# Expert weights by one register-addressed transfer per tile, and weights packed into few loads, in a two-layer macaron transformer block

## The reference

```python
x = x + 0.5 * _L0_ffn_ref(_layernorm(x), ...)    # attention, then 8 experts of which each token uses one
x = x + _L0_attn_ref(_layernorm(x), ...)         # causal attention, 16 heads of 8
x = x + 0.5 * _L0_ffn_ref(_layernorm(x), ...)    # the same weights as the first
x = x + 0.5 * _L1_ffn_ref(_layernorm(x), ...)    # dense FFN 128 -> 512 -> 128, low-rank addition, twice
x = x + _L1_attn_ref(_layernorm(x), ...)
x = x + 0.5 * _L1_ffn_ref(_layernorm(x), ...)

def _L0_ffn_ref(x, ...):
    hn = _layernorm(x, ln1_g, ln1_b)
    ...                                          # attention without a mask, 16 heads of 8, added to x
    hn2 = _layernorm(x, ln2_g, ln2_b).reshape(-1, h)
    idx = jnp.argmax(hn2 @ gate_w + gate_b, axis=-1)
    mid = relu(einsum('th,ehf->etf', hn2, w1) + b1[:, None, :])    # w1: 8 x 128 x 512
    y = einsum('etf,efh->eth', mid, w2) + b2[:, None, :]           # w2: 8 x 512 x 128
    return x + y[idx, arange(tokens)].reshape(b, s, h)
```

## Time and profile before

| | |
|---|---|
| time, median of 3 runs | 1058.04 us (1056.2 to 1064.72) |
| span of the profiled execution, first to last instruction | 1059.5 us |
| instructions | 25454 |
| TensorE matmul busy | 913.9 us (86%) |
| VectorE busy | 783.4 us (74%) |
| ScalarE busy | 676.3 us (64%) |
| GpSimd busy | 341.6 us (32%) |
| mean granted TensorE clock | 0.952 |

### The profile page before, as it was taken

The page is one execution under the profiler, slowest core; times in us unless marked ns, Lnnn a source line. Parts: engine busy times, 40 slices in busy tenths (PEclk is TensorE's granted clock), DMA queues, the critical chain, the costliest instruction groups (busy, mean ns, idle before and its releaser), DMA issues.

```text
span 1059.5 us, 25454 instructions
## 1 busy us (share of the span) xinstructions
PE 913.9 (86%) x10040; PEld 486.6 (46%) x10040; DVE 783.4 (74%) x1424; ACT 676.3 (64%) x1471; POOL 341.6 (32%) x603
## 2 busy tenths in 40 slices
PE   2599999898768799999999998987798889899997
PEld 1122333235757445554323332357675544555464
DVE  4789989964436977888999999635555697878646
ACT  2188877777546477777798876875452147767631
POOL 3444411342646323323233313426451032301100
PEclk9689999999969899999999999999798989999999
DMA  6123482001122321121021100101211122110000
GB/s 190 41 55 90 102 175 34 13 12 45 54 70 82 84 58 33 38 64 41 24 57 28 42 3 12 38 18 42 79 48 28 33 62 58 34 38 4 3 21 20
DMA packets 75384, 52.29 MB, mean 49 GB/s; under 512 B 16546, under 2 KB 72642, under 8 KB 75266
## 3 DMA queue, kind: packets, MB, share of 16 engines
q1 hardware_dynamic: 63700, 39.88, 14.7%
q10 hardware_dynamic: 8622, 4.75, 2.1%
q0 software_dynamic: 2944, 6.05, 1.7%
HBM read 13.64 MB, written 11.06 MB: 23 GB/s over the span
## 4 chain that ended last, share of the span: by engine, by line
PE 50%; DVE 22%; ACT 11%; issue 10%; DMA 2%; POOL 2%; another core or an unknown queue 1%; SPq 1%; DVEq 1%; POOLq 0%; ACTq 0%
PE ps L588 13%; PE ps L662 12%; DVE negm L968 9%; ACT pt L798 7%; DVE blockm L959 4%; PE ps L726 3%; PE ps L712 3%; PE ps L618 3%; PE ps L718 3%; PE ps L732 3%; PE ps L594 2%; PE ps L622 1%; PE ps L670 1%; PE ps L680 1%
## 5 line engine op out<-in xcount | busy, mean ns | idle before, releaser
L798 ACT ACTIVATE pt<-ps 128x512 f32<-128x512 f32 (+1 forms) x896 | 457.6, 566 | 167.8 <-PE ps L588 119.0
L968 DVE TENSOR_REDUCE negm<-ps 128x2 f32<-128x1024 f32 x256 | 300.3, 1218 | 29.0 <-PE ps L588 25.7
L662 PE MATMUL ps<-pt,va 128*32 128x256 f32 (+1 forms) x4352 | 276.4, 343 | 13.0 <-ACT ot L804 5.2
L959 DVE TENSOR_REDUCE blockm<-ps 128x8 f32<-128x1024 f32 (+1 forms) x192 | 195.4, 1041 | 41.5 <-PE ps L588 27.2
L588 PE MATMUL ps<-ks,qs 61*128 61x128 bf16 (+2 forms) x1536 | 172.9, 292 | 42.2 <-DVE negm L968 19.8
L588 PE MATMUL ps<-qs,ks 64*128 64x128 bf16 (+3 forms) x1408 | 169.0, 297 | 10.5 <-ACT parts L780 2.9
L662 PEld LDWEIGHTS ps<-pt,va 128*32 128x32 f32 x4352 | 92.5, 109 | 124.6 <-issue 82.7
L588 PEld LDWEIGHTS ps<-ks,qs 61*128 61x128 bf16 x1536 | 54.7, 95 | 196.1 <-issue 88.1
L1250 POOL CAST mpart<-negm 128x16 bf16<-128x16 f32 x64 | 13.2, 206 | 291.5 <-DVE negm L968 125.7
L833 ACT ACTIVATE stage<-ps,pt 128x128 f32<-128x128 f32 x240 | 68.5, 370 | 49.7 <-PE ps L712 37.3
L588 PEld LDWEIGHTS ps<-qs,ks 64*128 64x128 bf16 x1408 | 58.2, 95 | 67.6 <-ACT pt L798 43.4
(11 more groups left out here) (167 smaller groups left out, 1036.5 us busy)
## 6 DMA issues: line engine op xcount, KB each, us to landing
qs<-parts SPq DMA_DIRECT2D x80, 128.0 KB
ks<-parts SPq DMA_DIRECT2D x75, 128.0 KB
experts<-in_L_ffn_w SPq DMA_DIRECT2D x16, 256.0 KB
sorted<-stage ACTq DMA_DIRECT2D x4, 967.5 KB, 7.5
qs<-mrow SPq DMA_DIRECT2D x128, 6.0 KB
pt<-y_rows SPq DMA_DIRECT2D x8, 256.0 KB, 3.1
qs<-parts SPq DMA_DIRECT2D x32, 56.0 KB
ks<-parts SPq DMA_DIRECT2D x30, 56.0 KB
```

Source lines behind the costliest of these rows:

```text
L662: ins = pe.matmul(pv_bank[32 * j:32 * j + 32, q0:q1], va[n % 2][:, kb, value_at(g, j):value_at(g, j) + 32], pt[:, k_, from_:from_ + q1 - q ...
L798: a.activation(pt[:, k_ % NPT, S * s:S * s + width], b_bank(o + s)[:, 0:width], ACT.Exp).then_inc(b_free, 1)
L959: v.tensor_reduce(blockm[:, g % 2, :, t, PLACES[c_]], pair_of(ka)[:, :, 0:width].rearrange("p s (b c) -> p s b c", c=P), AX, ALU.max, nega ...
L968: v.tensor_reduce(negm[:, g % 2, :, t, c_], pair_of(ka), AX, ALU.max, negate=True).then_inc(a_free, 1)
```

## The change

Three things change together. First, the inputs are laid out on the host: all weights and biases of the attentions and the gate in one array, the experts' weights as one row of 1156 floats per partition and expert, the dense FFN's weights already transposed, the low-rank factors of an expert side by side. They come by five packed transfers: three column ranges of one array at the start (two on SP's queue, one on ACT's) and the dense FFN's two halves in batch 2. With that go `wflip`, `perm`, `gates`, `load`, four of the six `flip` jobs, and the permuting of q's and k's weights.

Second, the tile `experts` is gone. `lay` is now a job of SP: with the same waits, SP loads the expert number into a register and issues one transfer from device memory into the ring place; `up` waits for that transfer, on one semaphore per ring place. The ring keeps three places and the plan keeps the due times of `lay`.

Third, the start is reordered: statistics and rstd of batch 1 and the clearing of buffers come right behind the norm of batch 0, VectorE's memsets come before that norm, and for batch 0 ACT's queue issues four of the stacks and SP eight (before: six and six).

```diff
-HEAD = [("stats", 0), ("rstd", 0), ("norm", 0), ("hT", 0), ("q", 0), ("qrem", 0), ("k", 0), ("krem", 0), ("qmid", 0),
-        ("kmid", 0), ("qlo", 0), ("klo", 0), ("clear", 0), ("v", 0), ("stats", 1), ("rstd", 1), ("norm", 1)]
+HEAD = [("stats", 0), ("rstd", 0), ("norm", 0), ("stats", 1), ("rstd", 1), ("clear", 0), ("hT", 0), ("q", 0), ("qrem", 0),
+        ("k", 0), ("krem", 0), ("qmid", 0), ("kmid", 0), ("qlo", 0), ("klo", 0), ("v", 0), ("norm", 1)]
+ON_ACT = [(1, 5), (1, 1), (1, 4), (1, 2)]
...
-    first += [(14.2 + 0.15 * f, "flip", f, None) for f in range(FLIPS)] + [(15.2, "perm", 0, None)]
+    first += [(14.2 + 0.3 * f, "flip", f, None) for f in range(FLIPS)]
...
-        experts = sb("experts", [P, E, WE])
+        wpk = sb("wpk", [P, C_ALL])
...
                 elif name == "up":
                     need(pe, b_free, at_b[("tt", n, at)] + 1)
-                    pe.wait_ge(laid, number_of(n, at) + 1)
+                    need(pe, laid[number_of(n, at) % NWE], 16 * (number_of(n, at) // NWE + 1))
...
-                elif name == "lay":
-                    need(v, w_rest, 16 * len(rest))
-                    need(v, pv_done, at_pv[final_pv(last_batch(n), 3)] + 1)
-                    if tile_before(n, at, NWE):
-                        need(v, a_free, at_a[("dn", *tile_before(n, at, NWE))] + 1)
-                    v.tensor_copy(we[:, number_of(n, at) % NWE, :], experts[:, bass.ds(next_expert[n], 1), :]
-                                  .rearrange("p o c -> p (o c)")).then_inc(laid, 1)
...
         def sync_program(sp):
             for ev in plan:
                 name, n, at = ev
-                if name == "load":
-                    dst, src = rest[n]
-                    sp.dma_start(dst, src, allow_slow_non_contiguous=True).then_inc(w_rest, 16)
+                if name == "lay":
+                    r = number_of(n, at) % NWE
+                    need(sp, owner_step, 3 * (n + 1))
+                    need(sp, pv_done, at_pv[final_pv(last_batch(n), 3)] + 1)
+                    if tile_before(n, at, NWE):
+                        need(sp, a_free, at_a[("dn", *tile_before(n, at, NWE))] + 1)
+                    k_ = SLOTS * (n % 2) + at
+                    which = sp.value_load(owner[0:1, k_:k_ + 1], min_val=0, max_val=E - 1)
+                    sp.dma_start(we[:, r, :], d["experts"][bass.ds(which, 1), :, :].rearrange("o p c -> (o p) c"))\
+                        .then_inc(laid[r], 16)
...
         @block.sync
         def _(sp):
             x_tiles = d["L0_attn_x"].rearrange("b (i p) d -> p (b i) d", p=P)
             sp.dma_start(x[:, 0:TB, :], x_tiles[:, 0:TB, :]).then_inc(x_loaded, 16)
-            for dst, src in wl:
-                sp.dma_start(dst, src, allow_slow_non_contiguous=True).then_inc(w_loaded, 16)
+            sp.dma_start(wpk[:, C_FIRST:C_NEXT], d["weights"][:, C_FIRST:C_NEXT]).then_inc(w_next, 16)
             sp.dma_start(x[:, TB:TB * NB, :], x_tiles[:, TB:, :]).then_inc(x_rest, 16)
-            for dst, src in w_in_loads:
-                sp.dma_start(dst, src).then_inc(w_in_loaded, 16)
+            sp.dma_start(wpk[:, C_NEXT:C_ALL], d["weights"][:, C_NEXT:C_ALL]).then_inc(w_rest, 16)
...
         @block.scalar
         def _(a):
+            a.dma_start(wpk[:, 0:C_FIRST], d["weights"][:, 0:C_FIRST]).then_inc(w_loaded, 16)
             a.wait_ge(const_first, NFIRST)
             a.activation(a_tmp[:, 0:1], zero_col[:, :], ACT.Exp).then_inc(table_loaded, 1)
-            a.wait_ge(w_loaded, 16 * len(wl))
-            a.wait_ge(set_dve, SET_DVE)
             act_program(a)
```

More of the change, by code:

```diff
@@ L201, in segment, with schedule @@
     return out
-def schedule(causal_of, loads):
-    first = [(-100.0, name, k, None) for name, k in HEAD] + [(-50.0, "stack", 0, which) for which in STACK]
+def schedule(causal_of):
+    first = [(-100.0, name, k, None) for name, k in HEAD] + [(-50.0, "stack", 0, which) for which in HEAD_STACK]
     first += [(at, "setup", i, None) for i, at in enumerate(SETUPS)]
-    first += [(-200.0 if i < LOADS_FIRST else LOADS_FROM + (i - LOADS_FIRST) * LOADS_EVERY, "load", i, None)
-              for i in range(loads)]
-    first += [(-0.9, "wflip", 0, None), (2.9, "gates", 0, None), *[(4.0 + hm, "pads", hm, None) for hm in range(4)], (8.0, "late", 0, None), (8.6, "late", 1, None)]
-    first += [(14.2 + 0.15 * f, "flip", f, None) for f in range(FLIPS)] + [(15.2, "perm", 0, None)]
+    first += [*[(4.0 + hm, "pads", hm, None) for hm in range(4)], (8.0, "late", 0, None), (8.6, "late", 1, None)]
+    first += [(14.2 + 0.3 * f, "flip", f, None) for f in range(FLIPS)]
     plan = []
@@ L409, in program @@
         owner_step = sem("owner_step")
-        laid = sem("laid")
+        laid = [sem(f"laid{r}") for r in range(NWE)]
         prefilled = sem("prefilled")
@@ L563, in last_use, with need_layer @@
             return ("gate", l, None) if l < 8 else ("fu1", l, FB - 1)
+        def need_layer(eng, n):
+            need(eng, w_rest if n >= 4 else w_next, 16)
         def number_of(hm, t):
@@ L805, in act_program @@
                 elif name == "stack":
-                    if at[0] == 1 and n == 0:
+                    if n == 0 and at in ON_ACT:
                         stack(a, n, at)
@@ new lines @@
+    biases = [(a["L0_ffn_bq"], a["L0_ffn_bk"], a["L0_ffn_bv"], a["L0_ffn_bo"]),
+              (a["L0_attn_b_q"], a["L0_attn_b_k"], a["L0_attn_b_v"], a["L0_attn_b_o"]),
+              (b_in[0:P], b_in[P:2 * P], b_in[2 * P:3 * P], a["L1_attn_b_out"])]
+    columns = [heads_first(projections[0][0]), heads_first(projections[0][1])]
+    columns += [heads_first(biases[j][c]).reshape(P, 1) for j in range(3) for c in range(2)]
+    columns += [a[f"L0_ffn_ln{i}_{c}"].reshape(P, 1) for i in (1, 2) for c in ("g", "b")]
@@ new lines @@
+    columns += [projections[0][2], projections[0][3], everywhere(biases[0][2]), everywhere(biases[0][3]),
+                a["L0_ffn_gate_w"], everywhere(a["L0_ffn_gate_b"]), everywhere(a["L1_ffn_top_k_values"])]
+    for j in (1, 2):
+        columns += [heads_first(projections[j][0]), heads_first(projections[j][1]), projections[j][2],
+                    projections[j][3], everywhere(biases[j][2]), everywhere(biases[j][3])]
+    packed = {
+        "L0_attn_x": a["L0_attn_x"],
+        "weights": np.concatenate(columns, axis=1),
+        "experts": np.concatenate([a["L0_ffn_w1"], a["L0_ffn_w2"].reshape(E, FB, P, P).swapaxes(1, 2).reshape(E, P, F),
+                                   a["L0_ffn_b1"].reshape(E, FB, P).swapaxes(1, 2),
+                                   np.broadcast_to(a["L0_ffn_b2"].reshape(E, 1, P), (E, P, P))], axis=2),
+        "ffn": np.concatenate([a["L1_ffn_wi_w"].T,
+                               a["L1_ffn_wo_w"].T.reshape(FB, P, P).swapaxes(0, 1).reshape(P, F)], axis=1),
+        "lora": np.concatenate([a["L1_ffn_lora_As"], a["L1_ffn_lora_Bs"].swapaxes(1, 2)], axis=2),
+        "L1_ffn_top_k_indices": a["L1_ffn_top_k_indices"],
+    }
```

222 lines of the change are left out of this document (64 added, 158 removed).

## The result

The changed kernel takes 1138.7 us (median of four runs, 1137.1 to 1140.0), the kernel before in the same session 1058.0: a ratio of 1.074, 95% interval 1.071 to 1.078. The forecast was 1097, its range ended at 1128. The direction came as forecast, and so did the ring's turn and the seam; the loss is twice the forecast's. The profiled span went from 1059.5 to 1137.4, +77.9. The medians are 80.7 apart. Where span and time of one execution are both on record, the span is 1.8 to 1.9 less; so the profiled execution before took about 1061, an estimate, some 3 above its median, not the 1.5 of the forecast.

A forecast was written before the change was run, and what follows sets the result against it. TensorE, busy 86% of the span, was taken as the bound: time is won or lost where it waits. Expert stages +50.9, less 6, 3.6 and 2, made +39.3 on 1059.5, 1.5 above the median: 1097 us, range 1066 to 1128.

The forecast's parts named there:

- the ring's turn: Expert stages: up(t+3) follows up(t+1) by 2.34 + 4.6, two tiles in 6.94 us; three places act as two.
- the seam: Between the two expert groups: the first lay waits on SP's queue behind both result loads; 3.6 + 4.6 us to next up.
- The sum: Whole kernel: 50.9 lost in the expert stages, less 6, 3.6 and 2 saved, +39.3 us on the profiled 1059.5.
- Second groups: Second 15 tiles per layer: layer 1 takes 54 us, with stacks between lays adding about 5; layer 2 takes 49.0.
- First group, layer 1: First 15 tiles: up(0) at 254.2, up(2) +4.4, up(4) +11.3, up(14) +46.0, last add 3.9 later, at 304.1.
- Wrong: Signs against the forecast: landings under 2.7, lays before yloads, 2 us tiles, half clock, unexplained 10 us waits staying on top.
- L: Ring filling, from place free to weights there: 4.6 us, between 3.6 and 5.7; 28 us of time per us.
- The savings: Outside the expert stages: 6 us at the start, 3.6 from fewer flips, 2 from dropped expert loads.
- The clock falls too: Rival, expert groups: TensorE's waits drop its clock to 1.2 GHz, 43 us more, 1140 at most; chance 0.10.
- Hidden after all: Rival, ring filling: the 578 KB land early enough, only the savings remain, 1046 us; chance 0.08.
- short landing: Rival, ring filling: 578 KB land as fast as 256 KB, filling takes 3.6 us, time 1069; chance 0.12.

The follow-up runs named there:

- e1: Changed kernel, but the eight experts stay in on-chip memory and VectorE copies weights into the ring as before: 1051.6 us, ratio to before 0.992.
- e4: Changed kernel with GpSimd's eight scatters of rows in each second routing spread among the scatters of results: 1132.1 us.
- e5: Changed kernel with unused matmuls on TensorE in its waits for weights: 1136.5 us.
- e11: Changed kernel with both the scatters spread and TensorE's waits filled with unused matmuls: 1128.8 us.
- e3: Changed kernel, but each transfer into the ring brings 578 of the 1156 columns, half the bytes: 1118.0 us.
- e2: Changed kernel with six ring places instead of three, in memory of their own, queue orders unchanged: 1075.8 us.
- e9: Changed kernel with four ring places instead of three, in memory of their own, nothing else: 1098.3 us.
- e6: Changed kernel with the seam's two loads of results moved behind the next group's first three lays on SP's queue: 1131.2 us.
- e7: Changed kernel with six ring places, lays as early as their place allows, loads and adds of results later: 1038.0 us, ratio to before 0.980.
- e10: e7 with the eight scatters of each second routing spread among the scatters of results: 1041.7 us, ratio to before 0.982.

## Why the prediction was wrong

**The sum.** By the profiled spans the forecast was +39.3 and +77.9 came. Its terms beside the rows: first `up` behind attention's last matmul 5.1 for 4.6, twice: +1.0. First groups 62.3 and 63.5 for 49.9: +26.0. Seams 9.1 and 9.5 for 8.2: +2.2. Second groups 61.5 for 54.0 and 54.7 for 49.0: +13.2. All outside the expert stages -15.1 (10.4 ahead of them, 1.7 and 3.0 behind; the 3.0 go with the clock, see e1) for -11.6: -3.5. Together 38.9 of the missing 38.6.

**The failing step** is the one headed "First group, layer 1", and with it its copies in the other three groups: up(14) at +46.0 and the tail behind it. The four groups took 242.0 us where the forecast had 202.8, 39.2 more. Three things were wrong or missing in that step.

First, what the forecast listed under "Wrong" as waits of 10 us that no row explains: they stayed on top. In the kernel before they lay in the seam, beside the load of sorted rows, and were priced at nothing as covered. In the changed kernel the seam is elsewhere and they stand inside the first groups, beside GpSimd's run of scatters. e4 takes the run away, and the four groups are 16.7 shorter.

Second, the clock, which the sum put at nothing and left to a rival. It was 0.78 to 0.91 in the groups; e5 fills the waits, and the groups are 7.6 shorter. Both edits together (e11) give 23.7.

Third, the chain was started on the wrong tile. Three places are free at first, so tile 3 is the first that waits. Timeline of e11, `up` of tiles 0, 3, 13 and 14:

```profile
243.83 1.25 PE L668 MATMUL ps<-hTm,pt 128*128 128x128 f32 x8 [1.89 <-DMA pt<-in_experts]
...
253.73 1.16 PE L668 MATMUL ps<-hTm,pt 128*128 128x128 f32 x8
...
289.83 1.16 PE L668 MATMUL ps<-hTm,pt 128*128 128x128 f32 x8
...
293.44 1.13 PE L668 MATMUL ps<-hTm,pt 128*128 128x128 f32 x8 [1.56 <-DMA pt<-in_experts]
```

Tile 3 comes at +9.9, five turns lead to tile 13, and tile 14 follows 3.6 behind, at +49.6 (layer 2: +10.1 and +50.0). The forecast had its chain on the even tiles, with tile 14 at its end at +46.0: 3.6 and 4.0 too early. 1.4 of that is the turn, 7.2 for 6.94 five times; the rest is the miscounted tile. In e11's four groups what is left above the forecast is 15.5 (3.7, 4.5, 4.0 and 3.3; in the 4.5 are the stacks between the lays, which no run takes apart).

The 23.7 and the 15.5 make the 39.2 by construction, as both are read from e11; each size rests on one run of its kernel. With the seams' 2.2 and the first landings' 1.0 that is the 42.4 which the expert stages took beyond the forecast.

**L** was right: 4.72 for 4.6 in the turn shown. Its slope, 28 us per us, lies between what e3 gives by the time and by the stages, 26 and 34. The register load took less than assumed, add to issue 0.75 for 0.9, the landing more, 3.97 for 3.7. Right too were the ring of three acting as two (e2, e9) and the seam's mechanism (e6), though what the two seams are worth was under half of their length, 7.5 of 18.6: VectorE's add was next.

**The savings** were 7 to 9.3 for 11.6 (e1): 4.8 of 6 at the start, and the rest near 4 of 5.6.

**The rivals.** *The clock falls too* happened by the rows (0.78 to 0.91 in the groups, 0.66 in the seam) but its price of up to 43 us was wrong: e5 lifted the clock to 0.92 to 1.00 there, and the groups gained 7.6. The Trainium skill (TensorE: Matmul & The Clock Gate, section HAM oscillation) has the fall itself right: it speaks of loops in which waits for DMA let the clock drop. That fall hardly set the time here: in a loop whose turn is mostly the filling of a place (4.7 of 7.1 us) the slower matmuls mostly used up wait, and 7.6 of 242 us came back with the clock. *Hidden after all* and *short landing* are out by L.

## What to carry to other kernels

A ring that is filled by transfers needs its places counted by waits: with N places and the freeing of one tile's place behind the next tile's work, at best N - 1 tiles share the turn of freeing and filling, here 7.1 us (four places took 2.67 us a tile, not 2.4); three places cost 63 us more than six, which need three quarters of the memory that the resident weights gave back. A chain of such turns is counted from the first tile that waits. A wait that no row explains and that lies in a seam today is priced at zero only as long as the seam stays where it is. And a transfer moved onto a queue inherits everything that stands ahead of it there: give the queue the early work first, then look what waits behind it on the next engine (e6, e7).

## What the hardware did that was not expected

While GpSimd issued eleven indirect scatters in a row, 1.26 us apart, ScalarE and VectorE went on with finished TensorE work 2 and then 4 to 6 us late, both at the same moment (295.3 and 295.4; 791.4 and 791.5). With at most six in a row (e4, e11) no such wait appears; with ten and nine (e10) some are left. GpSimd's run as the cause is shown by that; what between the engines is held up by it is not, and no run here tells.

In the turns shown landing grew by 0.79 us for 289 KB (e3). That is 0.0027 us per KB on a fixed part of some 2.4 (3.97 less 1.58), an estimate from two transfers. With more than one fill under way the whole L read up to 6.5 us (e9).

SP's load of an expert number into a register took 0.27 us (median of 60 on SP; longest 0.99), less than the 293 and 501 ns of the kernel before.

The stretch behind layer 2's last add, with the same 2936 matmuls, took 271.2 us at a mean granted clock of 0.98 in the changed kernel and 276.0 at 0.95 in e3, which does not edit it.
